# Ranks, rows, step 1's transposes and late units in other places, and three x remainders on GpSimd in place of VectorE

## The chip, the core and the metric

The kernel runs on one NeuronCore of a Trainium2 chip. A core has five engines with an instruction queue each: TensorE (PE in the profile; PEld is its weight load) multiplies matrices, VectorE (DVE) and ScalarE (ACT) do elementwise work, GpSimd (POOL) does general work and issues DMAs, SyncE (SP) issues DMAs. Each queue is worked off in order, and the engines wait for one another through semaphores. The metric is the device time of one execution in microseconds (us); lower is better.

## The reference, cut to what matters

```
def _L0_cond_ref(inputs, initial_state):
    rates = jax.nn.relu(inputs) * DT
    c = initial_state[:, None, :] + jnp.cumsum(rates, axis=1)
    fl = jnp.floor(c)
    prev = jnp.concatenate([jnp.floor(initial_state)[:, None, :], fl[:, :-1, :]], axis=1)
    return (fl - prev) / DT

def _L1_cond_ref(x, t_emb, router_W, router_bias, w1, w3, w2, W1e, W2e):
    # x: 16 x 256 tokens of 256 channels; 8 experts, 2 of them per token
    shared = jax.nn.silu(xf @ w1) * (xf @ w3) @ w2          # 512 hidden channels
    s = jax.nn.sigmoid(jnp.concatenate([xf, tf], axis=-1) @ router_W)
    _, topk_idx = jax.lax.top_k(s + router_bias, K)
    gates = s_sel / (denom + 1e-09)
    h = jax.nn.gelu(jnp.einsum('nc,ech->enh', xf, W1e), approximate=False)
    y = jnp.einsum('enh,ehc->enc', h, W2e)
    routed = jnp.einsum('ne,enc->nc', combine, y)
    return (shared + routed) / (N_SHARED + K)

x = x + _L0_cond_ref(x, cond_1024)
x = x + _L1_cond_ref(x, cond_1024, ...)
```

The first layer adds spikes to x (the result is called x1), the second adds a mixture of experts: a shared network for all 4096 tokens, and for each token two of eight experts, weighted by gates.

## The kernel before, in words

The 4096 tokens are cut into 8 **groups** of 512 (NG = 8), the program into three parts: the shared network of groups 0 to 3, the experts for all tokens, and the shared network of groups 4 to 7. There are 4 **routes** of 1024 tokens (two groups each, RT = 8 tiles of 128 tokens): for each, the tokens' two experts are chosen, and their rows are scattered to lists in device memory, one list for each expert.

Products are made of two parts. An fp32 value v is split into v_hi (rounded to the fast fp32r format, by ScalarE) and **v_lo = v - v_hi** (the remainder), and a product is the sum of three: hi*hi, lo*hi and hi*lo (`three`, L1217 to L1219). For x1 of a group this is `x_hi` (ScalarE, `split`, L553) and `x_lo` (VectorE, `split_lo`, L1010; group 0 in two halves, L1020). There is one x_hi and one x_lo for all groups: they are overwritten when PE is through with the group before.

**PE's order in `shared(g)`** is: wait for x_lo of the group; four `up` products (each 12 matmuls of 512 columns, two halves of 6), four `down` products of the hidden rows (`hid`), each 4 matmuls of 256 columns that the trace shows as 8 records, and between them what belongs to routing: `to_rows(g, r)` turns x1 to token-major rows and makes the router's logits (L1260, L1261), and `ranks(r)` (L1272 to L1274) counts, with a triangular matrix, for each token of route r its rank in its expert's list. ranks(r) waits for VectorE's `prefix` of that route (L869). For group 2, ranks(1) stands between the halves of up(2, 3); to_rows(2, 1) stands before down(1, 1).

**VectorE** makes the hidden rows of the shared network (hid, L1133, silu from ScalarE times the other up product), and in between a long stream of small operations written out in `stream()`: the front layer's scans and sums (L759 to L783), `choose(r)` (the two experts, ending in the prefix), `place(r)` (slots from ranks) and `tile_list(n)`. The tables FILL and EXPERT_FILL give each place a credit in us; the stream is drawn until it is used up, so the order is fixed when the program is built and does not depend on what is ready. `finish(g)` (L1036) adds the down products of a group to its rows.

**ScalarE** splits x and the weights, makes silu and gelu and copies rows out of PSUM (`copy_rows`, L570). Its order is written out in `beside(g, at)`.

**GpSimd** has one queue in order: `add_w(k)` and `load_w(k)` are plain DMAs for the weights (L402, L397), `scatter(r, first, end)` issues two indirect DMAs for each tile t of route r (L434, rows to the experts' lists), `scatter_y(s)` two for each expert step (L449, results to y_rows). Each waits for a step of PE (`shared_step`, `half_step`), so that they are spread over the program. Before the change GpSimd does no elementwise work after its first 4 us, apart from these DMAs.

**The experts** run in 36 steps of two tiles of 128 slots. Step s on PE is: `to_channels(s)` transposes the tiles loaded from the lists into a PSUM bank `ps_x` (L1370); up products of step s-1 (L1217 to L1219 with `parts`), which wait for xt_lo of that step (VectorE, L1156); transposes of the gelu of step s-2 (L1411); down products of step s-3, which wait for ht_lo (VectorE, L1172); then `experts_beside(s)`. Step 1's bank is ps_d[0], which also holds the down products of group 3 until finish(3) has read them; so step 1 waits for finish(3) (s_base). ranks(2) stands at the end of step 1, ranks(3) at the end of step 8.

**The late groups** 4 to 7 run as groups 0 to 3, without routing. VectorE adds here the experts' results to the rows, 16 `unit`s of 4 operations each (L1054), which wait for their rows from y_rows. `fill_late` says at which place of which group each unit stands: place 2b is right behind the hidden row hid(g, b), place 2b + 1 behind it and, for b = 3, behind x_lo of the next group.

## Time and profile before

| | us |
|---|---|
| median of 3 runs | 338.25 |
| lowest and highest of them | 337.38, 339.94 |
| the profiled execution | 337.02 |
| its span, first to last instruction | 334.9 |

```profile
PE 306.2 (91%) x1948; PEld 277.5 (83%) x1948; DVE 218.1 (65%) x512; ACT 172.7 (52%) x303; POOL 156.5 (47%) x180
PE   0599999989998799879999899999999989999995
DVE  4888879789878998459744344544431197866662
POOL 3401115878864047546777777777777200000000
PEclk9999999997999999979999999999999999999999
```

The first line is busy time, share of the span and number of instructions of each engine. The others cut the span into 40 slices of 8.4 us; each digit is an engine's busy share in tenths, 9 being 90% or more. PEclk is the granted clock of TensorE in tenths: it is below full in two slices, the tenth and the eighteenth. Groups 0 to 3 are the first twelve slices or so, the experts follow to slice 31, groups 4 to 7 are the rest.

### The profile page before, as it was taken

Reading aid. Unit: us, or ns where it says so; the run is one execution under the profiler, and the core shown is the slowest. Engines: PE = TensorE matmul, PEld = TensorE weight load, DVE = VectorE, ACT = ScalarE, POOL = GpSimd, SP = SyncE. Lnnn points to the kernel's source line nnn. Section 1 sums busy time; section 2 is a strip of 40 time slices with the busy share of each in tenths; the row PEclk is TensorE's granted clock in tenths of the full one; section 3 lists DMA queues with packets and bytes.
Section 4 is the critical chain, followed back from the end, with each engine's and each line's share of the span. In section 5 each row is a group of like instructions: output and inputs, shape, how many; then the busy total and the mean of one; then the engine's idle time right before and its main releaser. Section 6 shows DMA issues by size and latency. Waiting matters only on the chain.

```text
span 334.9 us, 6758 instructions
## 1 busy us (share of the span) xinstructions
PE 306.2 (91%) x1948; PEld 277.5 (83%) x1948; DVE 218.1 (65%) x512; ACT 172.7 (52%) x303; POOL 156.5 (47%) x180
## 2 busy tenths in 40 slices
PE   0599999989998799879999899999999989999995
PEld 0488888868886699879999899999999868888884
DVE  4888879789878998459744344544431197866662
ACT  5759863973667475835555465756555211212020
POOL 3401115878864047546777777777777200000000
PEclk9999999997999999979999999999999999999999
DMA  6899665467996335433676565555322489847011
GB/s 188 166 360 205 170 140 162 134 203 162 307 185 206 98 95 143 146 112 120 169 221 208 181 216 176 171 177 173 135 104 110 135 297 339 284 154 219 2 63 63
DMA packets 36353, 57.79 MB, mean 173 GB/s; under 512 B 7520, under 2 KB 22880, under 8 KB 36320
## 3 DMA queue, kind: packets, MB, share of 16 engines
q1 hardware_dynamic: 27056, 30.03, 30.4%
q0 software_dynamic: 9264, 27.34, 27.3%
q8 instruction: 18, 0.29, 0.4%
q14 instruction: 15, 0.12, 0.1%
HBM read 33.15 MB, written 24.20 MB: 171 GB/s over the span
## 4 chain that ended last, share of the span: by engine, by line
PE 70%; DVE 12%; issue 6%; DMA 5%; POOL 3%; ACT 3%; SPq 1%; DVEq 0%; POOLq 0%; ACTq 0%
PE ps_d L1244 14%; PE ps L1217 12%; PE ps L1219 12%; PE ps L1218 12%; POOL x_slots L434 2%; PE ps L1411 2%; PE ps_d L1411 2%; PE ps L1370 2%; PE ps_t L1217 1%; DVE front L777 1%; PE ps_d L1370 1%; PE ps_r L1219 1%; DVE x L783 1%; PE ps_t L1219 1%; PE ps_r L1217 1%
## 5 line engine op out<-in xcount | busy, mean ns | idle before, releaser
L434 POOL DMA_INDIRECT x_slots<-base,slot_i x64 | 68.0, 1063 | 40.8 <-issue 22.8
L1217 PE MATMUL ps<-w_hi,parts 128*128 x192 | 58.7, 306 | 3.7 <-DVE parts L1156 1.3
L1244 PE MATMUL ps_d<-w_down,works 128*128 128x256 f32 x240 | 56.3, 386 | 1.6 <-DVE works L1133 1.6
L1219 PE MATMUL ps<-w_lo,parts 128*128 x192 | 54.7, 285 | 0.0
L1218 PE MATMUL ps<-w_hi,parts 128*128 x192 | 54.4, 283 | 0.0
L1217 PE MATMUL ps<-x_hi,w_hi 128*128 128x512 f32 x128 | 54.0, 422 | 0.0
L1244 PEld LDWEIGHTS ps_d<-w_down,works 128*128 128x128 f32 x240 | 46.3, 195 | 8.8 <-DVE works L1133 2.0
L580 ACT ACTIVATE works<-ps 128x512 f32<-128x512 f32 x32 | 19.0, 594 | 65.9 <-PE ps L1219 64.2
L1219 PE MATMUL ps<-x_lo,w_hi 128*128 128x512 f32 x128 | 51.2, 400 | 0.0
L1218 PE MATMUL ps<-x_hi,w_lo 128*128 128x512 f32 x128 | 51.0, 398 | 0.0
L449 POOL DMA_INDIRECT y_rows<-front,y_row x40 | 39.2, 981 | 12.2 <-issue 10.4
L1217 PEld LDWEIGHTS ps<-w_hi,parts 128*128 128x128 f32 x192 | 36.8, 192 | 4.6 <-issue 4.6
L449 POOL DMA_INDIRECT y_rows<-works,y_row x32 | 31.5, 985 | 14.8 <-issue 7.9
L1218 PEld LDWEIGHTS ps<-w_hi,parts 128*128 128x128 f32 x192 | 36.9, 192 | 0.0
L1219 PEld LDWEIGHTS ps<-w_lo,parts 128*128 128x128 f32 x192 | 36.7, 191 | 0.0
L1133 DVE TENSOR_TENSOR works<-works,ps 128x512 f32<-128x512 f32 x30 | 20.5, 685 | 20.8 <-ACT works L580 20.7
L1219 PEld LDWEIGHTS ps<-x_lo,w_hi 128*128 128x128 f32 x128 | 24.3, 190 | 5.8
L1218 PEld LDWEIGHTS ps<-x_hi,w_lo 128*128 128x128 f32 x128 | 24.6, 192 | 5.2
L1217 PEld LDWEIGHTS ps<-x_hi,w_hi 128*128 128x128 f32 x128 | 24.5, 191 | 5.2
L1156 DVE TENSOR_TENSOR parts<-ps_d,parts 128x512 fp32r<-128x512 f32 x18 | 12.4, 686 | 18.6 <-ACT parts L701 18.6
L402 POOL DMA_DIRECT2D w_lo<-w_all x9 | 8.7, 966 | 32.0 <-ACT w_lo L540 31.9
L706 ACT ACTIVATE works<-ps 128x512 f32<-128x512 f32 x24 | 14.4, 599 | 17.1 <-PE ps L1219 17.1
(156 smaller groups left out, 645.8 us busy)
## 6 DMA issues: line engine op xcount, KB each, us to landing
xg<-x_slots SPq DMA_DIRECT2D x72, 129.0 KB
w_lo<-w_all POOLq DMA_DIRECT2D x9, 512.0 KB, 6.5
front<-y_rows SPq DMA_DIRECT2D x9, 512.0 KB, 5.5
x<-x_t SPq DMA_DIRECT2D x16, 256.0 KB, 5.1
xg<-w_all POOLq DMA_DIRECT2D x8, 512.0 KB, 7.7
out<-base SPq DMA_DIRECT2D x16, 256.0 KB, 2.8
xg<-y_rows SPq DMA_DIRECT2D x7, 512.0 KB, 4.7
x_slots<-zeros SPq DMA_DIRECT2D x1, 1024.0 KB, 8.7
```

Of the source, the lines that this page charges most:

```text
L434: nc.gpsimd.indirect_dma_start(x_slots, bass.IndirectOffsetOnAxis(ap=slot_i[:, k, r * RT + t:r * RT + t + 1], axis=0), base[:, rows_at(g) ...
L449: nc.gpsimd.indirect_dma_start(y_rows, bass.IndirectOffsetOnAxis(ap=y_row[:, 2 * s + u:2 * s + u + 1], axis=0), y_sb[s % YB][:, u * C:(u + ...
L580: nc.scalar.activation(act[:, b % 2, :], ps[2 * (b % 2)][:, :], ACT.Silu).then_inc(s_act, 1)
L706: nc.scalar.activation(gelu[:, (s - 1) % 2, :], up_bank[s - 1][:, :], ACT.Gelu).then_inc(s_ege, 1)
L1133: nc.vector.tensor_tensor(hid_of(g, b), act[:, b % 2, :], ps[2 * (b % 2) + 1][:, :], ALU.mult).then_inc(s_hid, 1)
L1156: nc.vector.tensor_tensor(xt_lo[s % 2].rearrange("p c s -> p (c s)"), ps_x[s % 2][:, :], xt_hi[s % 2].rearrange("p c s -> p (c s)").bitcas ...
L1217: nc.tensor.matmul(out, x_hi, w_hi, start=start, stop=False, skip_group_check=True)
L1218: nc.tensor.matmul(out, x_lo, w_hi, start=False, stop=False, skip_group_check=True)
L1219: return nc.tensor.matmul(out, x_hi, w_lo, start=False, stop=stop, skip_group_check=True)
L1244: last = nc.tensor.matmul(ps_d[t // 2][:, (t % 2) * C:(t % 2 + 1) * C], hid_of(g, b)[:, t * P:(t + 1) * P], w_down[:, b * C:(b + 1) * C], ...
L1370: last = nc.tensor.transpose(ps_x[s % 2][:, c * 2 * P + u * P:c * 2 * P + (u + 1) * P], xg[:, s % XR, u, c * P:(c + 1) * P], ident)
L1411: last = nc.tensor.transpose(ps_h[s % 2][:, m * 2 * P + u * P:m * 2 * P + (u + 1) * P], gelu[:, s % 2, u * C + m * P:u * C + (m + 1) * P], ...
```

## The change

1. `split_lo` of groups 1, 2 and 3 goes from VectorE to GpSimd: the one of group 1 behind add_w(2) and load_w(4), the one of group 2 behind the first four indirect DMAs of route 0, the one of group 3 behind the first four indirect DMAs of route 1. Groups 5 to 7 (and 4) stay on VectorE.
2. PE: ranks(1) goes behind the whole of up(2, 3); to_rows(2, 1) behind down(1, 1), and its copies on ScalarE behind split(2); ranks(2) to the end of step 2; ranks(3) into step 9, behind its up products.
3. Step 1's transposes go to the bank ps[3]; the wait for finish(3) goes to step 3.
4. The units stand at other places of the late groups: none before the end of group 4, the last behind the last hidden row.

```
-        ps_x, ps_h = [ps[0], ps_d[0]], [ps[2], ps_d[1]]
+        ps_x = [ps[0], ps[3]] + [ps[0], ps_d[0]] * (STEPS // 2 - 1)
+        ps_h = [ps[2], ps_d[1]]
...
+            def split_lo(g):
+
+                pool.wait_ge(s_xhi, g + 1)
+                nc.gpsimd.tensor_tensor(x_lo[:, :, :], x1k[g][:, :, :], x_hi[:, :, :].bitcast(F32),
+                                        ALU.subtract).then_inc(s_xlo, 1)
...
             for k in range(SHARED_CHUNKS, SHARED_CHUNKS + 3):
                 add_w(k)
                 load_w(k + 2)
-            scatter(0, 0, 4)
+                if k == SHARED_CHUNKS:
+                    split_lo(1)
+            scatter(0, 0, 2)
+            split_lo(2)
+            scatter(0, 2, 4)
             add_w(SHARED_CHUNKS + 3)
             load_w(SHARED_CHUNKS + 5)
             scatter(0, 4, RT)
             for k in range(SHARED_CHUNKS + 4, SHARED_CHUNKS + 6):
                 add_w(k)
                 load_w(k + 2)
-            scatter(1, 0, 4)
+            scatter(1, 0, 2)
+            split_lo(3)
+            scatter(1, 2, 4)
...
-                    if b == SB - 1 and g + 1 < NG and g + 1 != NS:
+                    if b == SB - 1 and NS < g + 1 < NG:
                         split_lo(g + 1)
...
-                n = {(4, 3): 0, (4, 4): 1, (4, 5): 2, (4, 7): 3, (5, 1): 4, (5, 3): 5, (5, 4): 6, (5, 5): 7,
-                     (5, 7): 8, (6, 1): 9, (6, 3): 10, (6, 5): 11, (6, 7): 12, (7, 1): 13, (7, 3): 14,
-                     (7, 5): 15}.get((g, at))
+                n = {(4, 7): 0, (5, 1): 1, (5, 3): 2, (5, 4): 3, (5, 5): 4, (5, 7): 5, (6, 1): 6, (6, 3): 7,
+                     (6, 4): 8, (6, 5): 9, (6, 7): 10, (7, 1): 11, (7, 3): 12, (7, 4): 13, (7, 5): 14,
+                     (7, 7): 15}.get((g, at))
...
-                if g == 2:
-                    up(2, 3, (0,))
-                    ranks(1)
-                    up(2, 3, (1,))
-                else:
-                    up(g, 3)
+                up(g, 3)
                 if g == 0:
                     to_rows(1, 0)
-                elif g == 1:
-                    to_rows(2, 1)
+                elif g == 2:
+                    ranks(1)
...
                 down(g, 1)
                 if g == 0:
                     to_rows(1, 1)
+                elif g == 1:
+                    to_rows(2, 1)
...
-                if s == 1:
+                if s == 2:
                     ranks(2)
...
-                elif s == 8:
-                    ranks(3)
...
-                    if s == 1:
+                    if s == 3:
                         pe.wait_ge(s_base, 2 * NS)
...
                     if s == 6:
                         to_rows(7, 1)
+                    elif s == 9:
+                        ranks(3)
```

GpSimd's queue between route 0 and route 1, before. The L434 rows are indirect DMAs of one tile's rows (first two: the last tile of route 0, behind them route 1), the L402 and L397 rows are the weights' DMAs.

```order
L434 DMA x_slots<-base,slot_i 34816x258 [waits x1_rows_copied,down_done]
L434 DMA x_slots<-base,slot_i 34816x258
L402 DMA w_lo<-w_all 128x1024 [waits minus_w_hi_made]
L397 DMA xg<-w_all 128x1024 [waits minus_w_hi_made]
L402 DMA w_lo<-w_all 128x1024 [waits minus_w_hi_made]
L397 DMA xg<-w_all 128x1024 [waits minus_w_hi_made]
L434 DMA x_slots<-base,slot_i 34816x258 [waits x1_rows_copied,up_done,slots_made]
L434 DMA x_slots<-base,slot_i 34816x258
L434 DMA x_slots<-base,slot_i 34816x258 [waits x1_rows_copied,down_done]
L434 DMA x_slots<-base,slot_i 34816x258
L434 DMA x_slots<-base,slot_i 34816x258 [waits x1_rows_copied,down_done]
```

The same place of the changed kernel:

```order
L435 DMA x_slots<-base,slot_i 34816x258 [waits x1_rows_copied,down_done]
L435 DMA x_slots<-base,slot_i 34816x258
L403 DMA w_lo<-w_all 128x1024 [waits minus_w_hi_made]
L398 DMA xg<-w_all 128x1024 [waits minus_w_hi_made]
L403 DMA w_lo<-w_all 128x1024 [waits minus_w_hi_made]
L398 DMA xg<-w_all 128x1024 [waits minus_w_hi_made]
L435 DMA x_slots<-base,slot_i 34816x258 [waits x1_rows_copied,up_done,slots_made]
L435 DMA x_slots<-base,slot_i 34816x258
L435 DMA x_slots<-base,slot_i 34816x258 [waits x1_rows_copied,down_done]
L435 DMA x_slots<-base,slot_i 34816x258
L447 TENSOR_TENSOR x_lo<-x_3,x_hi 128x1024 [waits x_hi_made]
L435 DMA x_slots<-base,slot_i 34816x258 [waits x1_rows_copied,down_done,slots_made]
```

The subtraction for group 3 stands behind the first four indirect DMAs of route 1. Between the subtraction for group 2 and this one stand 16 indirect and 6 plain DMAs.

PE at the end of step 8, before. L1217 to L1219 are the last of step 8's down products, then ranks(3), then step 9's transposes (ps_d<-mix,xg).

```order
L1217 MATMUL ps<-w_hi,parts 128x256
L1218 MATMUL ps<-w_hi,parts 128x256
L1219 REGISTER_ALU
L1219 MATMUL ps<-w_lo,parts 128x256
L1272 MATMUL ps_r<-member,earlier 128x64
L1273 MATMUL ps_r<-prefix,mask 128x64
L1274 MATMUL ps_r<-prefix,mask 128x8
L1370 MATMUL ps_d<-mix,xg 128x128 x4
```

And after, in step 9, behind its up products and ahead of the transposes of the gelu (ps_d<-mix,works):

```order
L1229 MATMUL ps<-w_hi,parts 128x256
L1230 MATMUL ps<-w_hi,parts 128x256
L1231 REGISTER_ALU
L1231 MATMUL ps<-w_lo,parts 128x256
L1284 MATMUL ps_r<-member,earlier 128x64
L1285 MATMUL ps_r<-prefix,mask 128x64
L1286 MATMUL ps_r<-prefix,mask 128x8
L1420 MATMUL ps_d<-mix,works 128x128 x4
```

ranks(3) has moved behind one set of transposes and one of up products.

VectorE in group 4, before: hidden rows (L1133), units (L1054), x_lo of group 5 (L1010) and finish(4) (L1036).

```order
L1133 TENSOR_TENSOR front<-works,ps 128x512 x2
L1054 SCALAR_TENSOR_TENSOR base<-xg,gate,base 128x256 x4
L1133 TENSOR_TENSOR works<-works,ps 128x512
L1054 SCALAR_TENSOR_TENSOR base<-xg,gate,base 128x256 x4
L1054 SCALAR_TENSOR_TENSOR base<-front,gate,base 128x256 x4
L1133 TENSOR_TENSOR works<-works,ps 128x512
L1010 TENSOR_TENSOR x_lo<-x_1,x_hi 128x1024
L1054 SCALAR_TENSOR_TENSOR base<-front,gate,base 128x256 x4
L1036 SCALAR_TENSOR_TENSOR base<-ps_d,base 128x2x256 x2
```

And after:

```order
L1145 TENSOR_TENSOR front<-works,ps 128x512 x2
L1145 TENSOR_TENSOR works<-works,ps 128x512 x2
L1022 TENSOR_TENSOR x_lo<-x_1,x_hi 128x1024
L1066 SCALAR_TENSOR_TENSOR base<-xg,gate,base 128x256 x4
L1048 SCALAR_TENSOR_TENSOR base<-ps_d,base 128x2x256 x2
```

Four units stood in group 4; now one does, behind the four hidden rows and x_lo.

## Rows read from the trace of the kernel before

**Rows 1.** PE's waits: engine, line, releaser: us in total, times, longest us.

```profile
PE ps_t L1260 <- DVE x L783: 13.4, 3, 12.4
PE ps_r L1272 <- DVE prefix L869: 4.0, 3, 2.1
PE ps_d L1244 <- DVE works L1133: 1.6, 1, 1.6
...
PE ps_d L1370 <- DVE base L1036: 0.9, 1, 0.9
```

**Rows 2.** PE's timeline: start us, us, engine, line, operation, count [idle before <-releaser].

```profile
56.94 0.50 PE L1260 MATMUL ps_t<-mix,x 128*128 128x136 f32 x2 [0.43 <-DVE x L783]
...
60.53 0.48 PE L1217 MATMUL ps<-x_hi,w_hi 128*128 128x512 f32 x1
...
73.61 0.43 PE L1272 MATMUL ps_r<-member,earlier 128*128 128x64 f32 x2 [1.34 <-DVE prefix L869]
...
76.03 6.77 PE L1244 MATMUL ps_d<-w_down,works 128*128 128x256 f32 x24
82.44 0.58 PE L1217 MATMUL ps<-x_hi,w_hi 128*128 128x512 f32 x1
```

**Rows 3.** VectorE's timeline at the end of group 2.

```profile
78.37 1.21 DVE L1010 TENSOR_TENSOR x_lo<-x,x_hi 128x1024 fp32r<-128x1024 f32 x1
```

**Rows 4.** GpSimd's timeline, then busy time by stretch (engine busy, clock, DMA).

```profile
59.30 1.21 POOL L434 DMA_INDIRECT x_slots<-base,slot_i  x1 [0.30 <-issue]
...
84.70 0.97 POOL L434 DMA_INDIRECT x_slots<-base,slot_i  x1 [0.30 <-issue]
...
59.30:85.67 26.37, 25.03 (x112) 20.66 (x111) 22.24 (x63) 17.35 (x26) 21.80 (x22) 0.94 0.63 165
```

**Rows 5.** Timelines of ScalarE and PE at the end of group 0.

```profile
31.54 1.05 ACT L553 ACTIVATE x_hi<-x 128x1024 fp32r<-128x1024 f32 x1
...
37.29 0.58 PE L1217 MATMUL ps<-x_hi,w_hi 128*128 128x512 f32 x1
```

**Rows 6.** GpSimd's timeline at the program's start.

```profile
0.81 0.53 POOL L453 MEMSET mask<- 128x514 f32 x1 [0.29 <-POOLq L1471]
...
1.43 0.20 POOL L458 MEMSET mix<- 128x128 f32 x1
...
3.05 0.29 POOL L479 TENSOR_SCALAR_AFFINE_SELECT mix<-mix 128x128 f32<-128x128 f32 x1
```

**Rows 7.** PE's timeline in its first microseconds of work.

```profile
16.63 0.63 PE L1219 MATMUL ps<-x_lo,w_hi 128*128 128x512 f32 x1
17.06 0.58 PE L1217 MATMUL ps<-x_hi,w_hi 128*128 128x512 f32 x1
17.48 0.39 PE L1218 MATMUL ps<-x_hi,w_lo 128*128 128x512 f32 x1
17.71 0.39 PE L1219 MATMUL ps<-x_lo,w_hi 128*128 128x512 f32 x1
```

**Rows 8.** Step 8 to 9: VectorE, PE, and a stretch with its granted clock.

```profile
145.44 0.31 DVE L869 TENSOR_TENSOR_SCAN prefix<-same_e,member 128x72 f32<-128x72 f32 x1
...
145.80 0.43 PE L1272 MATMUL ps_r<-member,earlier 128*128 128x64 f32 x2 [2.13 <-DVE prefix L869]
...
147.17:150.58 3.41, 3.41 (x18) 3.41 (x17) 0.95 (x3) 1.32 (x3) 0.00 (x0) 0.50 0.56 146
```

**Rows 9.** Start of the experts: busy time by stretch (the third is VectorE's), PE's timeline.

```profile
104.58:116.86 12.28, 8.53 (x66) 7.38 (x64) 11.86 (x27) 7.29 (x12) 0.95 (x1) 1.00 0.33 100
...
117.00 0.38 PE L1217 MATMUL ps<-w_hi,parts 128*128 x1 [1.10 <-DVE parts L1172]
```

**Rows 10.** Group 4: timelines of ScalarE and VectorE.

```profile
269.57 0.60 ACT L580 ACTIVATE works<-ps 128x512 f32<-128x512 f32 x1 [3.92 <-PE ps L1219]
...
272.19 1.79 DVE L1054 SCALAR_TENSOR_TENSOR base<-front,gate,base 128x256 f32<-128x256 f32 x4
273.90 0.68 DVE L1133 TENSOR_TENSOR works<-works,ps 128x512 f32<-128x512 f32 x1
```

More of the change, by code:

```diff
@@ L622, in beside @@
                         make_rates(4, 1)
-                    elif at == 6:
-                        copy_rows(2, 1)
                     elif at == 7:
                         split(2)
+                        copy_rows(2, 1)
                         copy_rows(3, 0)
@@ L700, in experts @@
                         after(act_e, s_eup, s - 1)
-                        nc.scalar.activation(xt_hi[s % 2].rearrange("p c s -> p (c s)"), ps_x[s % 2][:, :],
+                        nc.scalar.activation(xt_hi[s % 2].rearrange("p c s -> p (c s)"), ps_x[s][:, :],
                                              ACT.Copy).then_inc(s_exhi, 1)
@@ L1155, in experts @@
                         after(dve, s_eup, s - 1)
-                        nc.vector.tensor_tensor(xt_lo[s % 2].rearrange("p c s -> p (c s)"), ps_x[s % 2][:, :],
+                        nc.vector.tensor_tensor(xt_lo[s % 2].rearrange("p c s -> p (c s)"), ps_x[s][:, :],
                                                 xt_hi[s % 2].rearrange("p c s -> p (c s)").bitcast(F32),
@@ L1369, in to_channels @@
                     for c in range(CC):
-                        last = nc.tensor.transpose(ps_x[s % 2][:, c * 2 * P + u * P:c * 2 * P + (u + 1) * P],
+                        last = nc.tensor.transpose(ps_x[s][:, c * 2 * P + u * P:c * 2 * P + (u + 1) * P],
                                                    xg[:, s % XR, u, c * P:(c + 1) * P], ident)
```

## The prediction

> **What bounds the kernel now.** I read the waits of PE first, then PE's timeline around each of them, then the queue of the engine that gets new work. PE is busy 91% of the span, so the table of waits shows nearly all that can be won: three late waits for the ranks' prefix, 4.0 us in total and 2.1 at the longest, one of 1.6 us for hidden rows of VectorE, one of 0.9 us for group 3's sums [rows 1]. In PE's timeline the reader is to see where shared group 2 starts (60.53), where group 3 starts (82.44), and that only one of these gaps, the ranks of route 1 at 73.61, lies between [rows 2]. Both group starts need x_lo. VectorE made x_lo of group 3 from 78.37 to 79.58, 2.9 us ahead of PE [rows 3]. So before, x_lo had slack, and moving it gains PE nothing by itself: what matters is how late the new maker is.
>
> The new maker is GpSimd, whose queue is in order. From 59.30 to 85.67 it runs 22 DMA instructions one behind the other, each indirect one followed by the next after 0.30 us; no one of them waits for another engine [rows 4]. That is a throughput chain of 26.37 us; the subtraction for group 2 is put ahead of its first instruction and the one for group 3 behind its last.
>
> **Part 1: x_lo of group 1.** GpSimd is idle when ScalarE ends x_hi at 32.59; PE wants x_lo at 37.29 [rows 5]. That leaves 4.7 us. Cost 0 unless one subtraction takes longer than that; if so, PE waits for the rest.
>
> **Part 2: what one subtraction (128x1024, two inputs) costs on GpSimd.** The trace has none. From below: a memset of 128 columns takes 0.20 us and one of 514 takes 0.53, so 0.85 ns a column and 0.09 us fixed, 1.0 us for 1024. From above: the one GpSimd operation that reads a tile takes 0.29 us for 128 columns [rows 6]; 1024 columns of it are 1.7 us if 0.09 are fixed and 2.3 if none are; with a second input read in turn, (0.29 - 0.09) x 8 x 2 + 0.09 = 3.3 us. I take 2.3, between the two, nearest the operation that also reads; both ends, 1.0 and 3.3, stay for the range. VectorE's 1.21 for this form [rows 3] is inside them. The Trainium skill (GPSIMD Engine Reference, 3.1 Elementwise — side-by-side cycle accounting) gives 4497 ns for a two-input operation of 2048 columns against 2293 on VectorE; half of it, as an estimate, is 2.25 us, and by it the sum below would be 0.1 us less. No run here shows it yet.
>
> **Part 3: x_lo of group 2.** It stands behind the fourth indirect DMA, in the place of the one that started at 59.30. It starts there and ends at 61.6. PE would be at group 2 at 60.53, or at 60.1, since the 0.43 us that PE waited for x1 of group 3 at 56.94 [rows 2] goes away with VectorE's subtraction ahead of it. So PE waits 1.5 us and the start moves from 60.53 to 61.7. GpSimd's chain moves by 2.3 + 0.3 = 2.6 us.
>
> **Part 4: x_lo of group 3.** The instruction that started at 84.70 now ends at 85.67 + 2.6 = 88.3; 0.3 later the subtraction starts, 2.3 later it ends: 90.9, and PE starts group 3 at about 90.95 in place of 82.44: **+8.5 us**. With 1.0 for a subtraction it is 88.3, +5.9; with 3.3 it is 92.95, +10.5. When would PE be there? Group 2 starts 1.2 later; the ranks of route 1 now stand behind the whole of up(2,3), whose second half is 1.4 us of matmuls (six at 0.23), which is just the 1.34 us that PE waited for prefix [rows 2]. Then 24 records of the down products follow. They took 6.77 us [rows 2], 1.2 more than 24 x 0.23, and may take 5.6 when PE has not stood before them. PE then comes at 81.0 to 82.2, and stands for 9 to 10 us. So the gain on the ranks of route 1 (1.3 us, and up to 1.7 of clock) is worth nothing: it ends in the wait for GpSimd. The same holds for part 3's 1.2 us. VectorE's freed 3 x 1.2 us is worth nothing either: it was not late for PE at either start.
>
> **Part 5: the restart.** After its wait of 12.4 us at the program's start [rows 1] PE's matmuls took 0.63 us each, started 0.43 apart, until about 17.1, and 0.39, started 0.23 apart, after that [rows 7]. From 12.4 on this is 4.7 us at half pace, 2.3 us lost. I take the same after 9 us of idleness: **+2.3** (bounds: one stretch of the low level as at 147.17, 3.41 us at a granted clock of 0.50, which is the 1.2 GHz level, 1.7 us lost [rows 8]; two such stretches, 3.4).
>
> **Part 6: ranks of route 2 and step 1's transposes.** The transposes of step 1 no longer wait for finish(3) (0.9 us), and the ranks go behind step 2. But VectorE is busy 11.86 of the 12.28 us from 104.58 to 116.86, in program order, and PE's next waits end on it, the last at 117.00 [rows 9]. Products of step 0 need xt_lo(0), which follows finish(3) on VectorE whatever PE does. So PE waits for parts in place of the two waits removed: **0** (at most 0.4, VectorE's idle time there). What hides it is VectorE; if VectorE were faster there, 1.5 us would come out.
>
> **Part 7: ranks of route 3.** PE stands for 2.13 us, from 143.67 to 145.80, until the prefix begun at 145.44 is there; then comes the stretch at 0.50 [rows 8]. The ranks now stand behind transposes and products of the next step, 0.4 + 1.4 us of work whose inputs are there (xt_lo of that step was made before the prefix). PE comes to them at 145.5 and waits 0.3. Gain 2.1 - 0.3 = 1.8, and 1.7 for the clock, which fell only after this gap: **-3.5** (bounds -1.8 and -3.8). VectorE asks for these ranks in place(3), which its stream (L1104 and L1105) puts 3.4 us of credit behind the prefix, more than a step's 3.2, so it should not wait.
>
> **Part 8: late units.** hid(4,3) was made at 273.90 although ScalarE's silu was ready at 270.17, since two units of 1.79 us stood ahead of it [rows 10]; PE waited 1.6 for it [rows 1]. Now no unit stands ahead of it. Gain **-1.6**. From group 5 on, the units stand in the gaps between hidden rows: two of 1.8 us with one hidden row of 0.7, 4.3 in all, in the 4.6 us of an up and a down product (12 and 8 records at 0.23). The last unit follows the last hidden row and lies beside three down products, 5.5 us of PE. Cost 0; without that cover the last unit would cost its 1.8.
>
> **Sum.** 8.5 + 2.3 + 0 - 3.5 - 1.6 = +5.7 us. The profiled execution took 337.02 us (span 334.9), so 342.7 for a profiled one. It lies 1.2 below the median of the runs, 338.25; on that the forecast is 338.25 + 5.7 = **344.0 us**, 1.7% slower.
>
> **The rivals.**
> A, the forecast: GpSimd's chain holds group 3 back by 7 to 10 us. Chance 0.68.
> B, the same wait with a cheap subtraction and a short restart: +5.9 + 1.7 - 3.5 - 1.6 = +2.5, 340.8 us, which is within 1%. For it speaks the memset's rate [rows 6]; against it the two inputs. It decides when a subtraction takes under about 1.5 us. Chance 0.16.
> C, a dear subtraction: 3.3 us or more, or one that has to wait for VectorE. VectorE is busy 22.24 of the chain's 26.37 us [rows 4], much of it with two-input operations of up to 1.2 us as in [rows 3]; waiting one out adds 1.2 to the chain. With 3.3 us and two low stretches: +10.5 + 3.4 - 5.1 = +8.8, and 1.2 for the wait, 348.3 us. Chance 0.09. The Trainium skill (SBUF — State Buffer, Who interferes with whom) states that a VectorE instruction with two SBUF inputs and a GpSimd instruction that reads SBUF exclude each other for their whole length; by that rule alone the forecast would become 345.2. No trace here shows it, since no GpSimd operation of that kind runs beside VectorE yet.
> D, faster: the subtraction is not held behind the indirect DMAs, because GpSimd's cores take it up beside them. Then x_lo of group 3 is ready at x_hi's end plus 2.3, about 80, PE starts group 3 at 81.0, and the gains stand: -1.5 - 3.5 - 1.6 = -6.6, 331.7 us. For it: GpSimd is busy 21.80 of the 26.37 us, so 4.6 us of its chain are gaps [rows 4]. Against it: the gaps are 0.30 us each and stand ahead of every indirect instruction, which is how a queue in order looks. It decides when x_lo comes before 81. Chance 0.07.
>
> **Numbers.** About 1% is what a measurement of this kernel can tell from no change. Slower by over 1% (above 341.6) holds A but its lower edge, and C: 0.74. Within 1%: B and that edge, 0.18. Faster: D, 0.08. The range takes in most of B and C: 339.5 to 348.5; A alone is 342 to 347.
>
> **What would show it.** Right: GpSimd's third subtraction starts behind four indirect DMAs of route 1 at 88 to 89; PE has a wait of 8 to 10 us before its first matmul of group 3, released by x_lo; the granted clock or the matmuls' spacing is at half behind it; PE's wait for the ranks' prefix near step 9 is under 0.5 us; no wait for hid(4,3); the waits at the experts' start still end on VectorE's parts. Wrong: a subtraction well outside 1.0 to 3.3 us, one that runs beside a DMA instruction, or a GpSimd chain that is shorter than 26 us because its instructions go quicker. A clock that does not fall after the long wait would take 2.3 off; one that falls elsewhere would add 1.7.

## The result and the profile after

The changed kernel takes 340.65 us (median of 6 runs, 338.99 to 341.29); the kernel before, in 6 runs of its own beside it, 339.1 (336.11 to 340.94). The ratio of the compared runs is 1.0106, with a 95% interval of 1.0072 to 1.0140: slower by 1.1%, some 3.6 us. A second comparison on another chip gave 1.0157 (1.0104 to 1.0210), some 5.3 us. The ratios compare the fast runs of each kernel only; the medians of all runs lie closer, 1.6 and 3.5 us apart. The forecast was 344.0 us, +5.7, with a range from 339.5 to 348.5.

The profiled execution of the changed kernel took 341.29 us, its span is 339.5 us, against 337.02 and 334.9 before.

First the page of the changed kernel: busy time, share of the span and instructions, then three of the rows in 40 slices.

```profile
PE 305.0 (90%) x1948; PEld 276.5 (81%) x1948; DVE 218.6 (64%) x509; ACT 173.0 (51%) x303; POOL 161.0 (47%) x183
PE   0599999995499779989999989999999999999995
POOL 3402415878827205756777776777777500000000
PEclk9999999999599999999999999999999999999999
```

VectorE has three instructions fewer, GpSimd three more. PE's row has a hole (5, 4) in the tenth and eleventh slices, and the two places where the clock fell before have become one, in the eleventh. The waits of PE in the changed kernel (engine, tile, line, releaser: us in total, times, longest us), in answer to [rows 1]:

```profile
PE ps_t L1272 <- DVE x L795: 13.0, 2, 12.4
PE ps L1229 <- POOL x_lo L447: 9.7, 2, 9.2
PE ps L1229 <- DVE parts L1168: 3.1, 3, 1.2
...
PE ps_r L1284 <- DVE prefix L881: 0.3, 1, 0.3
```

A wait of 9.2 us for GpSimd has come in; the waits for the prefix fell from 4.0 us to 0.3, and those for finish(3) and for hid(4,3) are gone. The wait for VectorE's parts of that line has grown to 3.1 us (1.3 before). PE's timeline (start us, us, engine, line, operation, count [idle before <-releaser]) shows where, in answer to [rows 2]:

```profile
61.38 0.50 PE L1229 MATMUL ps<-x_hi,w_hi 128*128 128x512 f32 x1 [0.43 <-POOL x_lo L447]
...
74.51 0.43 PE L1284 MATMUL ps_r<-member,earlier 128*128 128x64 f32 x2
...
89.86 0.79 PE L1229 MATMUL ps<-x_hi,w_hi 128*128 128x512 f32 x1 [9.24 <-POOL x_lo L447]
90.45 0.63 PE L1230 MATMUL ps<-x_hi,w_lo 128*128 128x512 f32 x1
```

The ranks of route 1 no longer wait, PE is through with group 2 at 80.62 (89.86 - 9.24), and then stands until 89.86, for a GpSimd result that was ready at 89.80 (the last row but one below). GpSimd's queue in the same stretch, in answer to [rows 4]:

```profile
58.89 2.44 POOL L447 TENSOR_TENSOR x_lo<-x,x_hi 128x1024 fp32r<-128x1024 f32 x1
61.48 0.98 POOL L435 DMA_INDIRECT x_slots<-base,slot_i  x1 [0.16 <-issue]
...
81.52 1.88 POOL L435 DMA_INDIRECT x_slots<-base,slot_i  x1 [0.30 <-issue]
83.70 1.00 POOL L435 DMA_INDIRECT x_slots<-base,slot_i  x1 [0.30 <-issue]
85.01 1.16 POOL L435 DMA_INDIRECT x_slots<-base,slot_i  x1 [0.30 <-issue]
86.47 0.96 POOL L435 DMA_INDIRECT x_slots<-base,slot_i  x1 [0.30 <-issue]
87.45 2.35 POOL L447 TENSOR_TENSOR x_lo<-x,x_hi 128x1024 fp32r<-128x1024 f32 x1
89.98 0.97 POOL L435 DMA_INDIRECT x_slots<-base,slot_i  x1 [0.17 <-issue]
```

ScalarE had made x_hi of group 3 by 77.1, and GpSimd comes to the subtraction at 87.45: the operands lie ready for 10 us while GpSimd works off its DMAs. Last, the stretch of the changed kernel in which the clock fell (busy time of PE, PEld, DVE, ACT and POOL with the number of instructions, granted clock, DMA share, GB/s):

```profile
83.33:93.57 10.24, 3.71 (x9) 2.93 (x10) 2.00 (x5) 2.24 (x3) 8.45 (x8) 0.50 0.94 257
```

The clock is at 0.50, the 1.2 GHz level, from 2.7 us after PE went idle to 3.7 us after it had gone on.

Followed through the program by PE's first matmul at each place, the loss and the gains are:

| place | before | after | difference |
|---|---|---|---|
| group 3 | 82.4 | 89.9 | +7.4 |
| experts, step 0 | 104.4 | 113.4 | +9.0 |
| step 8 | 138.3 | 147.3 | +9.1 |
| step 10 | 151.8 | 157.5 | +5.7 |
| group 4 | 255.1 | 261.5 | +6.4 |
| group 5 | 276.3 | 280.8 | +4.5 |
| span | 334.9 | 339.5 | +4.6 |

### The profile page after: what moved, and what is told of

Same layout as the page of the kernel before. It is cut to its first block, busy times and chain, and to the rows that moved or that the text cites. A ratio compares the mean times of both kernels' runs of the same rounds, so it can differ in the third digit from the quotient of the medians.

```text
span 339.5 us, 6757 instructions
## 1 busy us (share of the span) xinstructions
PE 305.0 (90%) x1948; PEld 276.5 (81%) x1948; DVE 218.6 (64%) x509; ACT 173.0 (51%) x303; POOL 161.0 (47%) x183
## 4 chain that ended last, share of the span: by engine, by line
PE 68%; POOL 8%; issue 8%; DVE 8%; ACT 4%; DMA 3%; SPq 1%; DVEq 0%; ACTq 0%; POOLq 0%
PE ps L1229 13%; PE ps_d L1256 12%; PE ps L1231 12%; PE ps L1230 12%; POOL x_slots L435 5%; PE ps L1420 2%; PE ps L1379 2%; PE ps_d L1420 2%; POOL x_lo L447 1%; PE ps_r L1231 1%; PE ps_t L1231 1%; PE ps_r L1229 1%; PE ps_t L1229 1%; PE ps_r L1230 1%; PE ps_t L1230 1%
## 5 line engine op out<-in xcount | busy, mean ns | idle before, releaser
L435 POOL DMA_INDIRECT x_slots<-base,slot_i x64 | 65.2, 1019 | 41.9 <-issue 22.2
L1229 PE MATMUL ps<-x_hi,w_hi 128*128 128x512 f32 x128 | 54.8, 428 | 9.7 <-POOL x_lo L447 9.7
L1229 PE MATMUL ps<-w_hi,parts 128*128 x192 | 58.1, 303 | 5.4 <-DVE parts L1168 3.1
L1256 PE MATMUL ps_d<-w_down,works 128*128 128x256 f32 x240 | 54.8, 379 | 0.0
L1230 PE MATMUL ps<-w_hi,parts 128*128 x192 | 53.8, 280 | 0.0
L1230 PE MATMUL ps<-x_hi,w_lo 128*128 128x512 f32 x128 | 51.8, 405 | 0.0
L1256 PEld LDWEIGHTS ps_d<-w_down,works 128*128 128x128 f32 x240 | 45.1, 190 | 6.3
L1229 PEld LDWEIGHTS ps<-w_hi,parts 128*128 128x128 f32 x192 | 36.2, 189 | 6.6 <-issue 6.6
L1230 PEld LDWEIGHTS ps<-w_hi,parts 128*128 128x128 f32 x192 | 36.3, 189 | 0.0
L771 DVE TENSOR_TENSOR_SCAN front<-mask,front 128x514 f32<-128x514 f32 x16 | 19.2, 1224 | 6.1 <-ACT front L535 6.0
```

The source lines that it names most:

```text
L435: nc.gpsimd.indirect_dma_start(x_slots, bass.IndirectOffsetOnAxis(ap=slot_i[:, k, r * RT + t:r * RT + t + 1], axis=0), base[:, rows_at(g) ...
L771: nc.vector.tensor_tensor_scan(sums[c], mask[:, :], rates[c], 0.0, ALU.mult, ALU.add).then_inc(s_scan[c], 1)
L1229: nc.tensor.matmul(out, x_hi, w_hi, start=start, stop=False, skip_group_check=True)
L1230: nc.tensor.matmul(out, x_lo, w_hi, start=False, stop=False, skip_group_check=True)
L1256: last = nc.tensor.matmul(ps_d[t // 2][:, (t % 2) * C:(t % 2 + 1) * C], hid_of(g, b)[:, t * P:(t + 1) * P], w_down[:, b * C:(b + 1) * C], ...
```

## The experiments

There were twelve runs, in three groups of four, each group on one chip together with the kernel before; the changed kernel itself ran in the third group only, so a number of it beside a run of the first two groups comes from another chip. On the chips of the first two groups every kernel, the one before too, took 25 to 30 us more, nearly all of it in the experts, so their ratios are to the 368.4 us and 364.8 us that the kernel before took there. What is known of this comes last in this section.

### Do the parts add up, and is it group 3's wait?

**All three subtractions back on VectorE**, the rest of the change kept:

```
-                if k == SHARED_CHUNKS:
-                    split_lo(1)
-            scatter(0, 0, 2)
-            split_lo(2)
-            scatter(0, 2, 4)
+            scatter(0, 0, 4)
...
-            scatter(1, 0, 2)
-            split_lo(3)
-            scatter(1, 2, 4)
+            scatter(1, 0, 4)
...
-                    if b == SB - 1 and NS < g + 1 < NG:
+                    if b == SB - 1 and g + 1 < NG and g + 1 != NS:
```

> The changed kernel with its three subtractions (x_lo of groups 1 to 3) back on VectorE, all else as changed. Queue theory (GpSimd's queue in order holds group 3's x_lo): the changed kernel's wait of 9.2 us ahead of group 3, the 0.4 us ahead of group 2 and about 1.6 us at the low clock behind it go, 11.2 us in all, so 4.5 us above before becomes 6.7 us below it, ratio 0.980. VectorE makes x_lo of group 3 about 1 us ahead of PE. Rival (the freed VectorE is where the change's gains come from, GpSimd's wait is only where they are spent): VectorE's 3 x 1.2 us come back on PE's path and the kernel lands only 3 us below before, ratio 0.991.

Measured: 365.70 us, 0.9904 of the kernel before (0.9860 to 0.9948). Without GpSimd's subtractions the change is a gain. The ratio is that of the rival (0.991) and not 0.980, but not for the rival's reason: VectorE's subtractions don't hold PE back, group 3 starts at 80.3. A new wait comes up in it: PE stands 3.6 us for rows that ScalarE copies, and ScalarE stands 3.5 us for a weight load. The kernel with only the third subtraction back, below, shows the same wait.

**Only the three subtractions on GpSimd**, the rest as before:

> The kernel before with the three subtractions on GpSimd at the changed kernel's places and nothing else. Queue theory: group 3 starts when GpSimd is ready, at the same time as in the changed kernel, since the moved ranks gain nothing ahead of that wait: 7.4 us for the start and 1.6 for the low clock behind it, 9 us above before, ratio 1.027. The wait itself is shorter than 9.2, since PE comes later. Rival (the moved ranks and rows of groups 1 and 2 did gain in the changed kernel): 11 to 12 us above before, ratio 1.034.

Measured: 379.05 us, 1.0266 (1.0147 to 1.0386). The edit is the mirror image of the one above. In its trace group 3 starts at 89.7 behind a wait of 8.0 us for x_lo. The time alone doesn't tell the two theories apart, since the interval holds both 1.027 and 1.034; that group 3 starts within 0.2 us of the changed kernel's 89.9 speaks for the first. The subtractions alone are the whole loss, and by the ratio more than the change's net.

**The changed kernel once more**, on the chip of the third group, with the kernel before traced there too:

> The kernel before, taken once more with a trace on the chip of the experiments. Expected: group 3's first matmul at 81 to 83 us and the first transposes of the experts at 104 to 105, as in the parts tried alone, which do not touch that place. If the experts' phase of every kernel is longer on this chip by the same 20 to 25 us, it shows here too, as waits of PE that no engine ends; if only the changed kernels showed them, they would be of the change.

> The changed kernel again, beside the others of this call. Expected 1.011 of the kernel before (+4 us), group 3's first matmul at 89.9. With this the parts tried alone add up or do not: remainders on GpSimd 1.027, group 1 and 2 moves 1.008, step 1 0.997, ranks(3) 0.994, units 0.997 multiply to 1.022; a result of 1.011 says that the parts are not additive: the wait for x_lo swallows the moves of groups 1 and 2 (1.027 x 0.994 x 0.997 x 0.997 = 1.014).

Measured: one run of the kernel before with a trace, 335.64 us; the changed kernel 340.92 us, 1.0157 (1.0104 to 1.0210). Group 3 starts at 81.1 and 89.1, +8.0. The 1.0157 is near the 1.014 at which the wait swallows the moves of groups 1 and 2, and 1.022, at which all parts would add up, lies just outside its interval; as the ratio of the subtractions alone is itself known to 1.2% only, this leans to the first and doesn't prove it. In the trace of the kernel before, the ranks of routes 1 and 3 wait as in [rows 2] and [rows 8]:

```profile
73.91 0.43 PE L1272 MATMUL ps_r<-member,earlier 128*128 128x64 f32 x2 [1.33 <-DVE prefix L869]
...
145.29 0.43 PE L1272 MATMUL ps_r<-member,earlier 128*128 128x64 f32 x2 [2.14 <-DVE prefix L869]
```

But the clock did not fall behind either of them. Two stretches of the same execution (columns as above):

```profile
68.00:100.00 32.00, 30.06 (x152) 25.32 (x151) 26.73 (x77) 19.27 (x34) 25.00 (x25) 1.00 0.82 208
140.00:160.00 20.00, 17.86 (x154) 17.65 (x154) 16.60 (x65) 10.41 (x20) 11.99 (x13) 1.00 0.45 149
```

So the same program with the same waits has the low clock in one execution and not in another. The spans of the kernel before in this group show it as well: 332.6 us at a mean granted clock of 0.999, 337.1 at 0.987.

**Step 1's transposes, ranks(3) and the late units alone**: remainders, ranks(1) and the rows of group 2 as before.

```
-        ps_x, ps_h = [ps[0], ps_d[0]], [ps[2], ps_d[1]]
+        ps_x = [ps[0], ps[3]] + [ps[0], ps_d[0]] * (STEPS // 2 - 1)
...
-                if s == 1:
+                if s == 2:
                     ranks(2)
...
-                elif s == 8:
-                    ranks(3)
...
                     if s == 6:
                         to_rows(7, 1)
+                    elif s == 9:
+                        ranks(3)
...
-                n = {(4, 3): 0, (4, 4): 1, (4, 5): 2, (4, 7): 3, (5, 1): 4, (5, 3): 5, (5, 4): 6, (5, 5): 7,
+                n = {(4, 7): 0, (5, 1): 1, (5, 3): 2, (5, 4): 3, (5, 5): 4, (5, 7): 5, (6, 1): 6, (6, 3): 7,
```

> Only step 1's transposes, ranks(3) and the late units are moved; remainders, groups 1 and 2 as before. If the parts add up: 0.9936 x 0.9966 x 0.9971 = 0.987 (about -4.7 us), faster than both. Rival: the gains share waits on VectorE and come out once only, 0.993. Group 3 starts at 81 to 82, late group 4 some 3 us earlier than in the kernel before.

Measured: 332.51 us (330.91 to 333.57), 0.9868 (0.9821 to 0.9914): some 4.5 us faster than the kernel before and the fastest of all. The product of the single parts, 0.987, is met, and 0.993 is outside the interval. It also gives the price of the rest of the change on this chip: 1.0157 / 0.9868 = 1.029, 9.9 us for the subtractions and the moves of groups 1 and 2 (each ratio is known to 0.5%; the medians are 8.4 us apart, the spans of the two traces 7.5). The waits of PE in this kernel:

```profile
PE ps_t L1261 <- DVE x L784: 13.4, 3, 12.4
PE ps L1218 <- DVE parts L1157: 3.0, 3, 1.2
...
PE ps_r L1273 <- DVE prefix L870: 1.7, 2, 1.4
```

The prefix of route 1 still costs 1.4, that of route 3 only 0.3, and PE waits for parts in place of finish(3). The places expected were missed: group 3 starts at 82.9, and group 4 at 253.5, only 0.2 us ahead of the 253.7 of the kernel before in its trace. Behind the wait for route 1 this execution has a low stretch (granted clock 0.50 from 76 to 78) that the traced one of the kernel before lacks, so this pair of traces, 2.0 us apart in span, shows less than the ratio of the runs does.

### The parts one by one

**ranks(3) moved alone.**

> The kernel before with only ranks(3) moved into step 9. Theory of the prediction: PE's wait of 2.1 us for the prefix falls to 0.3 and the low-clock stretch behind it goes, 3.3 to 3.5 us up to step 10; as the changed kernel showed 0.9 us more of waits for tiles at steps 20 and 21, some 2.5 us remain at the end, ratio 0.992. Rival (the gain is given back in full at the last stage, which GpSimd's queue sets): nothing remains, ratio 1.000.

Measured: 362.06 us, 0.9936 (0.9905 to 0.9966): -2.3 us.

**The late units moved alone.**

> The kernel before with only the units moved. Theory: the 1.6 us that PE waited for hid(4,3) go, and the work at the end stays hidden: 1.6 to 1.9 us, ratio 0.995. Rival (the last unit behind the last hidden row holds back the last stores): nothing or a loss, ratio 1.000 or more.

Measured: 363.01 us, 0.9966 (0.9937 to 0.9995), -1.2 us. The interval just leaves out 1.

**Step 1's transposes and ranks(2) alone.**

> The kernel before with only step 1's bank, its wait for finish(3) moved to step 3, and ranks(2) moved behind step 2. Theory (VectorE is the bound from 104.6 to 117): PE's waits for finish(3) and for the prefix go, waits for parts take their place, and the first step behind them starts within 0.4 us of where it did, ratio 1.000. Rival (these were PE's own waits): 1.5 us less, ratio 0.996.

Measured: 363.83 us, 0.9971 (0.9939 to 1.0003): it can't be told from nothing, nor from the rival's 0.996. PE's longest wait there is now one for VectorE's parts, 4.3 us. The waits have changed their name, as part 6 said.

**The moves in groups 1 and 2 alone** (ranks(1) behind up(2, 3), to_rows(2, 1) behind down(1, 1), its copies behind split(2)).

> The kernel before with only ranks(1) behind the whole of up(2,3) and to_rows(2,1) behind down(1,1) with its copies. Theory: here, with VectorE's x_lo in time, this is worth what the changed kernel could not use: 1.3 us of the wait for the prefix, 0.4 us at group 1's end if x1 of group 3 is there by then (VectorE's subtraction still stands ahead of it, so perhaps nothing), and 1.2 to 1.7 us of low clock: 2.5 to 3.4 us, ratio 0.991. Rival (the clock falls there whatever PE does, or VectorE's x_lo becomes the bound): 1.3 us or less, ratio 0.996.

Measured: 367.26 us, 1.0078 (1.0037 to 1.0118): a miss, slower where a gain was expected. Its trace has no wait for prefix at route 1 and starts group 3 at 80.8, against 81.2 to 81.7 in the three kernels above. By step 0 of the experts the gain is gone: it starts at 103.9, as two of those three do. At step 1 PE stands for finish(3), with VectorE as the releaser (us in total, times, longest us):

```profile
PE ps_d L1366 <- DVE base L1035: 3.5, 1, 3.5
```

That wait is no sign of the moves: the kernel with the units alone, which leaves this place as it was, stands there for 2.8 us on the same chip (more on this in the section on the slower chips). What is shown is that coming earlier to group 3 brings nothing by step 0. Why the whole costs 0.8% is not: there is no trace of the kernel before from that chip to set beside it.

### Where in GpSimd's queue can a subtraction stand?

**The third subtraction one tile (two indirect DMAs) earlier**:

```
-            scatter(1, 0, 2)
+            scatter(1, 0, 1)
             split_lo(3)
-            scatter(1, 2, 4)
+            scatter(1, 1, 4)
```

> The changed kernel with group 3's subtraction one tile (two indirect DMAs) earlier in GpSimd's queue. Queue theory: PE's wait falls by 2 x 1.27 = 2.5 us to 6.7, the time by 2.5, that is 2 us above before, ratio 1.006. Rival (what ends the wait is something else than GpSimd's place in its queue, x_hi or a DMA): no change in the wait, ratio 1.013.

Measured: 371.52 us, 1.0123 (1.0036 to 1.0211). PE waits 6.1 us for x_lo in place of 9.2, and group 3 starts at 86.7 in place of 89.9. 3.1 us less for two DMAs fits the spacing in the queue (83.70 to 86.47 is 2.77 for two in the changed kernel). The ratio doesn't settle how much of it reaches the end: the interval holds both numbers.

**Both subtractions early**: the second behind the first tile of route 0, the third behind the last DMA of route 0, ahead of two weights' loads.

```
-            scatter(0, 0, 2)
+            scatter(0, 0, 1)
             split_lo(2)
-            scatter(0, 2, 4)
+            scatter(0, 1, 4)
...
             scatter(0, 4, RT)
+            split_lo(3)
...
-            scatter(1, 0, 2)
-            split_lo(3)
-            scatter(1, 2, 4)
+            scatter(1, 0, 4)
```

> The changed kernel, subtractions still on GpSimd, but group 2's behind the first tile of route 0 and group 3's behind the last tile of route 0, ahead of four plain and four indirect DMAs. Queue theory: group 3's x_lo is ready 9 us sooner, at about 80.6, PE waits 0.5 us or less for it, and the time is that of the kernel with VectorE's subtractions within 1 us, ratio 0.980. Rival (a subtraction on GpSimd costs PE by itself, through VectorE's two-input operations that stand still beside it): 2 us or more above that kernel, ratio 0.986 or more.

Measured: 372.08 us, 1.0124 (1.0041 to 1.0207), where 0.980 was expected: the clearest miss. The wait for x_lo is gone as planned (group 3 starts at 82.2, 1.3 us of waiting). The loss has only moved. The load of the ninth weight chunk stands behind the subtraction, is issued at 82.70 in place of 77.8 to 78.8 in the other kernels, and ScalarE, in order too, stands for it. PE's waits in this kernel:

```profile
PE ps_t L1271 <- ACT base L582: 5.9, 2, 5.5
...
PE ps L1228 <- POOL x_lo L447: 1.3, 1, 1.3
```

and ScalarE's timeline:

```profile
91.56 1.06 ACT L551 ACTIVATE w_hi<-xg 128x1024 fp32r<-128x1024 f32 x1 [4.66 <-DMA xg<-w_all]
```

PE reaches step 0 of the experts at 112.3, only 1.1 us before the 113.4 of the changed kernel's trace. The rival of this run, that VectorE's standstill beside the subtraction costs PE, isn't separated by the time, which lies on its side of 0.986; the wait that the trace shows at this place is ScalarE's, for the load. At none of the places tried was GpSimd's queue free for 2.4 us: ahead of the weights' DMAs the subtraction delays them, behind the indirect DMAs it delays PE.

**Only the third subtraction back on VectorE**:

```
-            scatter(1, 0, 2)
-            split_lo(3)
-            scatter(1, 2, 4)
+            scatter(1, 0, 4)
...
-                    if b == SB - 1 and NS < g + 1 < NG:
+                    if b == SB - 1 and g in (2, 4, 5, 6):
```

> The changed kernel with group 3's remainder alone back on VectorE; groups 1 and 2 keep GpSimd. Theory one (the loss is group 3's wait for the third subtraction): group 3 starts at 81 to 83 in place of 89.9, and nearly all is won back, 0.990 of the kernel before, as with all three undone. Theory two (anything long in GpSimd's queue also delays the weights' loads behind it, and ScalarE stands for them): group 3 starts at 82 too, but the second subtraction still makes load_w(8) 2.4 us later than with all undone, ScalarE waits 5 to 6 us for it, PE waits as long for rows in group 3, and the ratio is 0.997 to 1.005.

Measured: 335.54 us, 0.9957 (0.9919 to 0.9995). Against the changed kernel beside it, 0.9957 / 1.0157 = 0.980, 6.6 us won by putting back one subtraction of 2.35 us (5.4 between the medians). That is the direct test of part 4. Where the rest of the 9.9 us stays, the trace shows the next wait, of 3.85 us, with a granted clock of 0.50 from 90 to 94 behind it. PE and ScalarE in this kernel:

```profile
90.58 0.79 PE L1270 MATMUL ps_t<-mix,x 128*128 128x136 f32 x2 [3.85 <-ACT base L581]
```

```profile
78.40 0.97 POOL L398 DMA_DIRECT2D xg<-w_all  x1
...
87.66 1.06 ACT L550 ACTIVATE w_hi<-xg 128x1024 fp32r<-128x1024 f32 x1 [3.59 <-DMA xg<-w_all]
```

The effect is theory two's, the cause it named is not. The load was issued at 78.40, when it is issued in the kernel before too (78.09), but could be used only 9.3 us later. In the kernel before on this chip:

```profile
78.09 0.98 POOL L397 DMA_DIRECT2D xg<-w_all  x1
...
85.60 1.06 ACT L539 ACTIVATE w_hi<-xg 128x1024 fp32r<-128x1024 f32 x1 [1.42 <-DMA xg<-w_all]
```

That is 7.5 us from issue to use. It landed late in the two kernels in which PE came to group 3 at 80.3 or earlier (this one and the one with all three undone, 87.66 and 87.86), and by 84.8 to 86.5 in the others that issued it between 77.8 and 78.8, although the one with only groups 1 and 2 moved came at 80.8. The DMA engines are all busy from 82 to 92 in the traces of both kinds. Whether another transfer got ahead of the load, and which, was not tested and stays open.

### The slower chips

On the first two chips the kernel before took 368.4 and 364.8 us, and the trace of the third shows it at 335.64. The kernels with one part alone and the remainders on VectorE begin step 0 at 103.9 to 107.5 there (the four with one part alone at 103.9 to 104.8, as the kernel before does at 103.9 here), but group 4 at 278.6 to 283.5 in place of 253.7. So the 25 to 30 us lie in the experts, in waits of PE that the profile puts down to nothing ("issue") or to engines that it then finds late. One of several such rows of the kernel with ranks(3) moved alone:

```profile
245.74 0.28 PE L1218 MATMUL ps_t<-w_hi,parts 128*128 x1 [0.86 <-issue]
```

Behind them stand mostly ScalarE's own. Its waits that the profile puts down to "remote" come to 58 to 69 us, nearly all in the experts, in each of the eight kernels of these two chips, and there is none in the six traces from the other chips. Two of them, in the kernel with the units alone:

```profile
106.97 0.60 ACT L701 ACTIVATE parts<-ps 128x512 fp32r<-128x512 f32 x1 [3.76 <-remote]
128.81 0.60 ACT L717 ACTIVATE works<-ps 128x512 f32<-128x512 f32 x1 [3.11 <-remote]
```

The first stands at the start of the experts. There PE has a wait of 2.7 to 5.6 us, for VectorE's parts or for finish(3), in seven of the eight kernels (the one with ranks(3) alone waits 0.95), and never over 1.3 us in the six traces from the other chips. So the waits of 4.3 us (step 1's transposes alone) and 3.5 us (groups 1 and 2 alone), and one of 4.7 us in the kernel with both subtractions early, are not to be read as costs of those edits.

What "remote" stands for here, and why these chips have it, was not looked into. It is common to all kernels there, so the ratios stand, but they were taken over other waits in the experts, and on such a chip a part that is worth something beside a wait of VectorE may be worth another amount.

## Why the prediction was right, and where its sizes were off

The side and the mechanism (rival A) came out as forecast. The time doesn't show that by itself: 340.65 is inside the range, but below A's own 342 to 347 and next to B's 340.8. It is the trace that decides for A, with a subtraction of 2.35 us, where B needed one under 1.5, and a wait of 9.24 us released by x_lo, where 9 to 10 was said. The first comparison gave +3.6 us and the second +5.3, for the +5.7 of the sum. Term by term, with the two pairs of traces (before and after in each):

| term | predicted | first pair | second pair |
|---|---|---|---|
| group 3 starts later (parts 1 to 4) | +8.5 | +7.4 | +8.0 |
| restart (part 5) | +2.3 | +1.6 | +0.7 |
| step 0 to 8 (part 6) | 0 | 0 | 0 |
| ranks(3) (part 7) | -3.5 | -3.4 | -1.9 |
| from there to group 4 | 0 | +0.8 | +0.5 |
| late units (part 8) | -1.6 | -1.9 | -1.9 |
| sum | +5.7 | +4.5 | +5.4 |

**Part 1, right.** x_lo of group 1 was ready at 36.5, before PE wanted it; no wait.

**Part 2, right.** A subtraction takes 2.44 and 2.35 us, and 2.97 for the first, beside VectorE; 2.3 was taken. The estimate of 2.25 from the Trainium skill (GPSIMD Engine Reference, 3.1) was 0.1 to 0.2 short of the second and third.

**Part 3, right in the main.** Group 2 started at 61.38 for 61.7. Its wait was 0.43 in place of 1.5, since PE came 0.9 late to group 1 already, by some matmuls of group 0 that went slower and a wait of 0.3 us at the end of that group. In the second pair group 2 starts at 60.8 before and 60.6 after, so this part cost nothing.

**Part 4, right in its mechanism, 0.5 to 1.1 us too large.** The indirect DMA expected to end at 88.3 ended at 87.43, and x_lo expected at 90.9 was there at 89.80. The subtraction doesn't pay the 0.30 us gap that every indirect DMA pays: it starts at 87.45, and the next DMA follows after 0.17. The chain behind the second subtraction also ran in 25.95 us (61.48 to 87.43) in place of 26.37. What the two pairs differ by is mostly in the starts of before: 82.4 holds one stretch of the low clock at 75.49 to 78.90, and 81.1 holds none. That the gain at the ranks of route 1 would be swallowed was right (PE through at 80.62, expected 81.0 to 82.2).

**Part 5, the term that was mis-sized.** 2.3 us was taken from the program's start, where all 4.7 us at half pace lie behind the wait. Here the clock fell 2.7 us into the wait and was at 0.50 for 10.24 us in all, of which only 3.7 fell on work: at most 1.85 us, and 1.6 measured. That is just under the lower bound given, 1.7. In the second pair 0.7 us remain, mostly because the kernel before waited 0.6 us for rows in group 3 there.

**Part 6, right.** The differences at step 0 and step 8 are the same, 9.0 and 9.1 (8.7 and 8.7). PE waits 1.19, 0.80, 1.07 and 1.11 us for parts, and VectorE is what it waits for. The part alone gave 0.9971, with 1 inside its interval, and 0.996, the rival's, too; the differences between the steps are the evidence.

**Part 7, right, but half of it is a matter of chance.** The remaining wait is 0.29 (0.3 predicted). The -3.5 was 1.8 of waiting and 1.7 of clock. The first pair gave 3.4, since the execution of before had the low stretch; the second gave 1.9, since that one had none. The part alone gave -2.3 us, between the two. The sum counted the second half as certain.

**From step 10 to group 4, a term that was missing.** 0.8 of the gain is given back at the tiles of steps 20 and 21 (0.5 in the second pair), where PE waits for rows loaded from the lists (xg, 0.26 and 1.43 us, against 0.73 before). A likely reading, which no run tests, is that PE comes there earlier relative to GpSimd's queue.

**Part 8, right.** No wait for hid(4,3), 1.9 for 1.6, and the last unit costs nothing.

**The rivals.** B (cheap subtraction) is out by 2.35 us against 1.5. D (taken up beside the DMAs) is out, since the third subtraction started 10 us after its operands were there. C's size is out, but the exclusion it speaks of is in the traces, and falls on the other engine. VectorE beside the first subtraction (33.54 to 36.51) and the second:

```profile
34.21 0.68 DVE L1145 TENSOR_TENSOR works<-works,ps 128x512 f32<-128x512 f32 x1
34.81 2.78 DVE L795 SCALAR_TENSOR_TENSOR x<-front,x 128x1024 f32<-128x1024 f32 x1
...
59.23 2.77 DVE L777 SCALAR_TENSOR_TENSOR front<-front,cond 128x257 f32<-128x257 f32 x2
```

The operation of L795 takes 1.22 us elsewhere, and here it ends 1.1 us after GpSimd's does; the pair of L777, otherwise 0.89, takes 2.77. The hidden row between them has one input in PSUM and takes its usual 0.68. So VectorE's operations with two inputs in SBUF wait for GpSimd's to end, as the Trainium skill states (SBUF — State Buffer, Who interferes with whom), while GpSimd lost at most the 0.6 us of its first. VectorE had slack at both places, so PE saw nothing of it. But it takes back nearly all that the move was worth to VectorE: three times 1.21 us taken off, 1.56 and 1.9 us put back, and in line with this VectorE's busy time did not fall (218.1 before, 218.6 after).

## What to carry to other kernels

Before work goes to an idle-looking engine, read its queue in order and not its busy share: GpSimd was 47% busy and the subtraction took 2.35 us, yet its result came 9 us late, because the DMAs ahead of it ran until 87.43, and when it was put ahead of the weights' DMAs it held up the weights instead. When several moves come in one change, try them apart: three of these parts gave 1.3% together, and one lost 2.7% alone (1.5 to 3.9). A gain from a clock that no longer falls should be counted as a possible one and not as certain, since the same wait in the same program brings the low clock in one execution and not in the next.

## What the runs showed of the hardware that was not expected

- A subtraction on GpSimd starts 0.02 us behind the indirect DMA instruction ahead of it, and the next DMA instruction follows after 0.16 to 0.17 us, where two DMA instructions are 0.30 apart.
- After waits of 1.3 and 2.1 us the granted clock fell to 0.50 for 3.41 us each in one execution, and in another of the same kernel it did not fall at all (span 334.9 and 333.5 us). After a wait of 9 us it fell in both traces of the changed kernel, already during the wait, and so it did in the wait of 3.85 us of the kernel with the third subtraction back.
- A load of 512 KB was used 7.5 us after its issue in one kernel and 9.3 in another, with the issue at the same time to 0.3 us.
- On two of the chips ScalarE waited 58 to 69 us for what the profile calls "remote", on the others not at all; the times of the kernel before differ by 25 to 30 us between them.
